# Where the last conditioning and two input roundings stand in a written-out order of work

## The reference, cut to what matters

```
x = x + attention(moe(x))          # 16 heads of 8 channels, rotary, causal
y = x @ W_base.T + b_base + 2 * sum_e w[b,e] * (x @ As[e].T) @ Bs[e].T       # L3_cond2, one matrix per sequence b
h = silu(y @ w1.T * s1) * (y @ w2.T * s2)
h = gelu(h @ h1.T * sh1)
h = gelu(h @ h2.T * sh2)
x = x + h @ w3.T * s3                                                        # L3_ffn, hidden width 512
```

## Time and profile before

| what | value |
|---|---|
| median of three runs | 1387.59 us |
| the profiled execution's own time | 1386.45 us |
| its span | 1384.6 us |
| TensorE matmul busy | 1248.2 us (90%) |
| TensorE weight load busy | 966.3 us (70%) |
| VectorE busy | 853.5 us (62%) |
| ScalarE busy | 667.4 us (48%) |
| GpSimd busy | 269.2 us (19%) |
| the chain that ended last | PE 71%, DVE 16%, ACT 7%, issue 4% |
| last attention, in the span | 1096 to 1248 us |
| last ffn, in the span | 1251 to 1384 us |

### The profile page before, as it was taken

How to read it: one execution, slowest core, us unless ns; L and a number is a source line. 1 busy time by engine, 2 the same in 40 slices (tenths; PEclk the granted TensorE clock), 3 DMA queues, 4 the chain that set the end, 5 groups by cost and what they waited for, 6 DMA issues and landing times.

```text
span 1384.6 us, 26311 instructions
## 1 busy us (share of the span) xinstructions
PE 1248.2 (90%) x9327; PEld 966.3 (70%) x9327; DVE 853.5 (62%) x1813; ACT 667.4 (48%) x1346; POOL 269.2 (19%) x379
## 2 busy tenths in 40 slices
PE   5899871889999899998999999899999999998999
PEld 2555530458878789887778887598889755556777
DVE  4989779564556566657776465556554566764242
ACT  2665676445434243453444444243444466655553
POOL 5666200110004143320000022233410211100000
PEclk9999995999999999999999999999999999999999
DMA  9000010501232123105025002032020000000000
GB/s 317 2 1 2 2 76 0 205 1 62 77 130 87 50 76 88 41 22 206 1 95 214 1 14 62 19 101 74 28 88 1 1 2 2 2 1 1 0 16 16
DMA packets 42892, 75.69 MB, mean 55 GB/s; under 512 B 3848, under 2 KB 33808, under 8 KB 41872
## 3 DMA queue, kind: packets, MB, share of 16 engines
q1 hardware_dynamic: 38672, 65.62, 13.1%
q0 software_dynamic: 4096, 8.40, 2.1%
HBM read 59.72 MB, written 14.29 MB: 53 GB/s over the span
## 4 chain that ended last, share of the span: by engine, by line
PE 71%; DVE 16%; ACT 7%; issue 4%; DVEq 1%; DMA 1%; POOL 0%; ACTq 0%; SPq 0%; POOLq 0%
PE bank L1811 7%; PE bank L1822 7%; PE bank L1807 7%; PE bank L1866 5%; PE bank L1798 4%; PE bank L1659 3%; PE bank L1586 3%; PE bank L1876 3%; PE bank L1591 3%; PE bank L1592 2%; PE bank L1593 2%; DVE SM L2251 2%; PE bank L1791 2%; PE bank L1793 2%; PE bank L1792 2%
## 5 line engine op out<-in xcount | busy, mean ns | idle before, releaser
L2059 ACT ACTIVATE SC<-bank 128x512 f32<-128x512 f32 x192 | 114.4, 596 | 223.0 <-PE bank L1807 125.1
L2146 DVE SCALAR_TENSOR_TENSOR SC<-bank,SM,SC 128x512 f32<-128x512 f32 x128 | 95.9, 749 | 121.8 <-PE bank L1811 100.2
L1822 PE MATMUL bank<-A,SC 128*128 x1024 | 137.7, 278 | 5.7 <-DVE SC L2146 5.1
L1807 PEld LDWEIGHTS bank<-X,SC 128*128 128x128 f32 x1024 | 126.8, 193 | 19.3 <-issue 12.5
L1811 PE MATMUL bank<-X,SC 128*128 128x128 f32 x1024 | 136.6, 276 | 3.3 <-DVE SC L2429 2.8
L1807 PE MATMUL bank<-X,SC 128*128 128x128 f32 x1024 | 136.6, 277 | 3.2 <-ACT SC L2043 2.5
L1822 PEld LDWEIGHTS bank<-A,SC 128*128 128x128 f32 x1024 | 126.3, 193 | 15.0 <-issue 14.1
L1811 PEld LDWEIGHTS bank<-X,SC 128*128 128x128 f32 x1024 | 124.5, 192 | 5.4 <-DVE SC L2429 5.2
L1866 PE MATMUL bank<-A 128*128 128x128 f32 x736 | 101.1, 281 | 12.1 <-DVE A L2579 8.8
L1960 ACT ACTIVATE A<-bank,SM 128x128 f32<-128x128 f32 x256 | 73.7, 381 | 64.8 <-DVE SM L2251 64.5
L1866 PEld LDWEIGHTS bank<-A 128*128 128x128 f32 x736 | 91.0, 195 | 17.2 <-ACT A L2084 8.6
(11 more groups left out here) (324 smaller groups left out, 2529.0 us busy)
## 6 DMA issues: line engine op xcount, KB each, us to landing
A<-in_moe SPq DMA_DIRECT2D x36, 768.0 KB, 10.1
A<-xs SPq DMA_DIRECT2D x20, 256.0 KB, 3.8
ys<-A SPq DMA_DIRECT2D x20, 256.0 KB, 2.4
BW<-in_l1f SPq DMA_DIRECT2D x2, 2048.0 KB, 7.6
BW<-in_l2f SPq DMA_DIRECT2D x1, 3456.0 KB, 12.0
BW<-in_l1c SPq DMA_DIRECT2D x1, 3072.0 KB, 17.9
BW<-in_l3f SPq DMA_DIRECT2D x1, 2816.0 KB, 9.8
A<-in_l1c SPq DMA_DIRECT2D x1, 2560.0 KB, 8.6
```

Of the source, the lines that this page charges most:

```text
L1807: m = e.matmul(at["pg"].ap[:, cut(q)], wx[:, cut(q)], x, start=True, stop=True)
L1822: m = e.matmul(o, at["h"].ap[:, cut(q)], W[:, bass.ds(r + (1024 + 128 * q), 128)], start=k == 0 and q == 0, stop=k == 1 and q == 3)
L2059: e.activation(at["h"].ap, at["pg"].ap, ACT.Gelu_apprx_tanh).then_inc(at["gelu"][0], 1)
L2146: return e.scalar_tensor_tensor(out=o, in0=a, scalar=s, in1=b, op0=o1, op1=o2)
```

## The change

```
-        seq = (items + flat(seq[12:]) + flat(mix(m3, f2, m4, shared_items())) + at3 + cond_items("y3b", 3, "x3")
-               + l3_ffn_items())
+        c3, l3 = cond_items("y3b", 3, "x3"), l3_ffn_items()
+        at3 = at3[:17] + c3[0:1] + at3[17:26] + c3[1:2] + at3[26:35] + c3[2:3] + at3[35:]
+        l3[0:2] = [(needs + [("x3", 3)], stages, gives) for needs, stages, gives in l3[0:2]]
+        seq = items + flat(seq[12:]) + flat(mix(m3, f2, m4, shared_items())) + at3 + l3[0:2] + c3[3:4] + l3[2:]
```

## The result

The changed kernel takes 1392.85 us, median of 20 runs (1387.93 to 1397.25), and the kernel before 1385.68 us, median of 20 (1381.04 to 1389.12). The ratio is 1.0056 [1.0043, 1.0068]: slower by 6.0 to 9.4 us, about 7.8. The forecast was 1391.9 us, +4.3 on the 1387.59 us of three runs of the kernel before.

A forecast was written before the change was run, and what follows sets the result against it. It took the last attention as a chain of latencies through ACT and DVE, bound by PE in its late part. The terms 4.0 + 2.8 - 3.1 + 0.6 = +4.3 on 1387.59 gave 1391.9 us, range 1384.0 to 1396.5.

The forecast's parts named there:

- the walk: Following three engines' queues through the last attention and tail: +4.3 us in all, 1391.9 us; held at 0.50.
- Place 17's mask 3.6 late, on DVE's subtraction: Chunk 0's insertion, places 16 to 17: mask waits for a bank, 3.6 us late, place 19 4.8; 4.0 us taken.
- Chunk 1, 2.8: Chunk 1's insertion between places 25 and 26: later masks stay 2.8 us late, since PE is the bound from there.
- Chunk 2 and the tail, the last mask 3.8 later: Chunk 2 between the last two heads: last mask 3.8 us later, yet X 1.45 earlier, apart from earlier lags.
- The first silu 3.1 earlier: Start of the last ffn: table load hidden in the wait, first silu 3.1 us earlier, apart from earlier lags.
- Chunk 3's Y among the silus, 0.6: Last ffn: chunk 3's Y on ACT now stands between the silus of chunks 0 and 1, costing about 0.6 us.
- rival 4: TensorE's clock falls once more, taking up to 1.7 us of PE: +6.0, 1393.6 us; chance 0.05.
- Rival 1: Both attention insertions fall into PE's and ACT's waits, only the tail counts: -2.5, 1385.1 us; chance 0.16.
- Rival 2: No bank or ACT order decides; each attention insertion costs PE's work, 2.2 us: +1.9, 1389.5 us; chance 0.14.
- Rival 3: The bubble in the attention does not shrink; each insertion costs 5.0 us: +7.5, 1395.1 us; chance 0.15.

The follow-up runs named there:

- e6: Kernel before with only chunk 0's conditioning moved between places 16 and 17; other chunks and roundings stay: ratio 1.0033.
- e4: Kernel before with only the two roundings moved ahead of chunk 3's conditioning, no conditioning among the heads: ratio 1.0011.
- e1: Changed kernel plus four unread products that keep TensorE busy in the tail's waits: 1393.42 us, ratio 1.0062.
- e2: Changed kernel with the inserted conditionings' products in banks of another ring, taking none from the scores: ratio 1.0035.
- e3: Changed kernel with the inserted conditionings' addition moved one turn later, behind the row maxima of the head before: ratio 1.0006.
- e7: Changed kernel with chunk 2's conditioning behind the last head instead of between the last two: ratio 1.0043.
- e12: e3 with the inserted conditionings' second product in a bank of the other ring: ratio 1.0003.
- e11: e3 with the four extra products of e1 in the tail's waits: ratio 1.0000.
- e9: e8 with chunk 3's scaling, product and addition as an item of their own ahead of the roundings: 1378.32 us, ratio 0.9957.
- e8: e5 with the addition of chunks 0 to 2 one turn behind their product, as in e3: ratio 0.9988.
- e5: Kernel before with both roundings, no longer waiting for X, and the ffn's first product ahead of chunk 3's conditioning: ratio 0.9998.

## Why the prediction was right, and where it was short

The forecast of 1391.9 us lies 0.95 under the median of 1392.85. That closeness is in part luck: the 1387.59 us of three runs, from which it starts, lie 1.91 above the median of 20, which made up for more than half of what the change, about +7.8, was over +4.3. Its case, the walk, held in its mechanism. Its steps:

- **Place 17's mask 3.6 late, on DVE's subtraction**: 3.68 late, released by L2256. Place 19 was given 4.8 and came 5.83 late in the profiled pair, in which a piece of half clock lies between masks 17 and 18 (0.88 in 1146 to 1160); in e6, without it, mask 19 is 4.78 late (70.63 against 65.85). What stays of chunk 0 is 3.83 (e6 against e4), forecast 4.0.
- **Chunk 1, 2.8**: 2.46.
- **Chunk 2 and the tail, the last mask 3.8 later**: from mask 34 to mask 35 it is 7.86 us, before 4.06 to 4.07: 3.8. From mask 34 to X it is 19.66, before 21.36: 1.70 shorter, where the walk gives 1.45.
- **The first silu 3.1 earlier**: at full clock (e1) it comes 19.66 + 5.26 = 24.92 us behind mask 34, before 28.34: 3.42 earlier. In the changed kernel it comes 26.44 behind it, and only 1.90 is left.
- **Chunk 3's Y among the silus, 0.6**: the first eight silus take 15.54 us instead of 14.37, that is 1.17 more; of that the distance from the first to the second, still at half clock, is 2.68 instead of 2.05, so 0.6 is clock and 0.5 the Y. (That ACT and DVE are "the bound" there is loosely put: the earlier trace rows has them busy 10.73 and 9.57 of 17 us, so it is the chain through them.)

At full clock the terms add to 3.83 + 2.46 - 3.42 + 0.54 = +3.4, against +4.3 forecast. What came on top is **rival 4**, the clock. In the profiled run it takes 1.52 us ahead of the first silu and 0.63 behind it, 2.15 together, where one piece was priced at up to 1.7 and held for 0.05 likely; the attention adds 0.46 (mask 34 is 6.75 late, not 3.83 + 2.46 = 6.29), the difference of a piece of 1.04 in the changed kernel and one of 0.59 in the kernel before (133.13 against 132.54 in e4). With these the terms give 3.41 + 2.15 + 0.46 = +6.02, where the stretch is +6.06. It is not a rival of the walk at all but a term beside it, and should have stood in the sum. The fall has its likely cause in the walk's own result: with the conditionings gone from the tail PE has 5.02 us of work in 1240 to 1248 and then waits 3.43 us for chunk 3's scaling, which the change put behind both roundings. All six kernels whose profiled run has this wait, 3.43 or 3.44 us (the changed kernel, e2, e3, e4, e7, e12) fall to half clock there, e4 with all three conditionings still in the tail, and with the two fillings (e1, e11) or the product ahead (e9) the clock stays up. But the wait isn't needed for a fall: e6 falls with 1.41 and 1.38 us. What of the emptied tail and the wait weighs how much isn't shown. The Trainium skill, TensorE: Matmul & The Clock Gate, Why this matters for your kernels, has the rule that TensorE falls to half rate when it idles too long between bursts; the trace agrees here (3.43 us of idling, the next product at 2.08 us instead of 1.12), and e6's 1.41 and 1.38 us show that shorter waits can stand before a fall too.

Over all runs the clock seems to weigh more than in the profiled pair. The kernel before has a mean granted clock of 0.9769 to 0.9782 on the four chips, the changed one 0.9728. Within one chip, runs of the kernel before differ among themselves by 1.0 to 1.4 us for each 0.001, and those of the changed kernel by 1.2 (lines through the runs), so the lower clock goes with some 5 to 6 us of the 7.8. The chips themselves differ: at a clock of 0.975 the lines put the kernel before at 1386.2 us on one and at 1391.3 on another, so times at equal clock can be compared on one chip only. On which of them the changed kernel ran is not known. On the chip of e1, which has the changed kernel's order with the filling, runs at 0.974 and 0.975 take 1391.2 us on average (2 runs) and those of the kernel before 1387.7 (6 runs): about +3.6, as between the lines at 0.975, near the +3.4 of the terms. That is a correlation from few runs, not an experiment, and e11, whose mean clock rose against e3's without a gain in the ratio, warns against taking it for a price; where the pieces beyond the tail's fall in the other runs stays open, since a trace is there of one run only.

- **Rival 1, the waits take it in**: wrong; masks 17 and 29 are 3.68 and 6.76 late. The Trainium skill, Perfetto Trace Analysis, Optimization Strategy, has it that interleaving regimes with different most-contended engines may improve performance; here each of the three interleavings cost time (2.60, 0.85 and 1.15 us at X), and the measurement decides.
- **Rival 2, PE's work alone, 2.2 each**: chunk 1 comes near it, chunk 0 does not. And taking out waits without any of the work took 2.1 us (banks) and 3.16 (the addition's place; 3.8 at full clock, e11) off mask 35: waits are a good part of the price.
- **Rival 3, 5.0 each**: wrong, although its 1395.1 us is not far off and its +7.5 is nearest to the ratio's +7.8. The difference alone would have picked it; the masks do not.

## What to carry to other kernels

A piece of work put into a loop of latencies costs the chain it hangs on, not its busy time: see which buffer of the ring it takes and behind what it stands in each in-order queue, and let a result be taken up one turn after it is ordered (here 3.5 us at X, for the same work). When work leaves a stretch where TensorE already waits, put a fall of its clock into the sum as a term, and fill the wait with products that are ready, as the fourth chunk's was. An early start of a stage is worth what the next item behind it allows: 6.5 us at the first silu became 0.4 at the end until chunk 3's product was ahead, and 5.7 then, of which 1.2 is the late addition's (e8 against e5).

## What the runs showed of the hardware

- The clock fell while TensorE was far from idle: in 1146 to 1160 of the changed kernel PE is busy 11.39 of 14 us, none of its waits is over 1.70 us, and the granted clock is 0.88. In e6 it fell to 0.50 in the tail with waits of 1.41 and 1.38 us before it, where the kernel before, with 0.41 and 1.38, kept 1.00.
- The same instructions meet a different clock in different runs: the attention that the changed kernel and e1 share had one piece at half clock in one profiled run and three in the other, 2.2 us at mask 35.
- The same kernel takes a different time at the same mean clock on different chips: before, at 0.975, 1386.2 us on one and 1391.3 on another, read from lines through 17 and 23 runs.
- At half clock a product of 128x512 takes 0.63 us instead of 0.39 in the ffn, and the conditioning's pair 2.08 instead of 1.12.
- The table load in front of the silu (1.28 us) starts while its activation still waits for PE, 4.83 us ahead of it (1249.34 and 1254.17).
